# A fused GRU and transformer block: other steps and another order for the side work of the attention stage

## The reference

```python
# GRU cell, scanned over the 128 positions
r = sigmoid(i_r + h_r); z = sigmoid(i_z + h_z); n = tanh(i_n + r * h_n)
h = (1.0 - z) * n + z * h
...
x1 = ln(x) * (1.0 + scale1) + shift1
q, k, v = split(x1 @ qkv_w + qkv_b)                 # 16 heads of 128
attn = softmax(einsum("bthd,bshd->bhts", q, k) * 128 ** -0.5)
a = einsum("bhts,bshd->bthd", attn, v) @ out_w + out_b
x = x + gate1 * a
x2 = ln(x) * (1.0 + scale2) + shift2
x = x + gate2 * (gelu(x2 @ ffn_w1 + ffn_b1) @ ffn_w2 + ffn_b2)
```

## Time and profile before

| | |
|---|---|
| median of 3 runs | 740.95 us |
| the profiled execution's own time | 741.54 us |
| its span | 739.7 us |
| TensorE busy | 711.7 us |
| VectorE busy | 575.7 us |
| ScalarE busy | 484.0 us |
| GpSimd busy | 104.1 us |
| attention stage | about 271 to 655 us |

### The profile page before, as it was taken

The page is one execution under the profiler, slowest core; times in us unless marked ns, Lnnn a source line. Parts: engine busy times, 40 slices in busy tenths (PEclk is TensorE's granted clock), DMA queues, the critical chain, the costliest instruction groups (busy, mean ns, idle before and its releaser), DMA issues.

```text
span 739.7 us, 25163 instructions
## 1 busy us (share of the span) xinstructions
PE 711.7 (96%) x10380; PEld 525.0 (71%) x10380; DVE 575.7 (78%) x1581; ACT 484.0 (65%) x1621; POOL 104.1 (14%) x134
## 2 busy tenths in 40 slices
PE   6889999999999999999999999999999999999997
PEld 5689888888888776666767667676676777644555
DVE  5667888888888878877878988888887888834643
ACT  4346666666655567776787777877777777775453
POOL 0222222222210001011001111011110111000040
PEclk9869999999999999999999999999999999999999
DMA  6311111211000302322222332223322233200001
GB/s 224 96 38 39 40 39 43 70 39 39 10 12 3 116 4 44 45 44 45 45 58 46 71 52 51 55 48 71 54 51 47 56 66 44 51 16 28 29 9 50
DMA packets 79017, 36.70 MB, mean 50 GB/s; under 512 B 70667, under 2 KB 73911, under 8 KB 78903
## 3 DMA queue, kind: packets, MB, share of 16 engines
q1 hardware_dynamic: 78327, 33.53, 20.4%
q10 hardware_dynamic: 576, 1.57, 0.6%
HBM read 16.20 MB, written 2.10 MB: 25 GB/s over the span
## 4 chain that ended last, share of the span: by engine, by line
PE 83%; DVE 6%; ACT 5%; DMA 2%; SPq 2%; issue 1%; POOL 0%; DVEq 0%; ACTq 0%
PE bank L527 20%; PE bank L529 19%; PE bank L528 19%; PE bank L635 12%; PE bank L643 5%; PE bank L547 5%; SPq L381 2%; DVE h_hi L1330 2%; ACT prob L1111 1%; PE bank L534 1%; ACT zg L1037 1%; DMA pT_lo<-p_lo 1%; DVE nu L1324 1%; DMA xr<-in_weights 1%; DVE mx L1402 1%
## 5 line engine op out<-in xcount | busy, mean ns | idle before, releaser
L635 PE MATMUL bank<-h_hi,whh_hi 128*128 128x16 f16 x1536 | 111.5, 178 | 8.6 <-DVE h_hi L1330 7.2
L635 PEld LDWEIGHTS bank<-h_hi,whh_hi 128*128 128x128 f16 x1536 | 90.0, 97 | 30.2 <-DVE h_hi L1330 26.0
L635 PE MATMUL bank<-h_hi,whh_lo 128*128 128x16 f16 x1536 | 109.9, 177 | 1.5 <-issue 1.5
L1111 ACT ACTIVATE prob<-bank,nmx 128x128 f32<-128x128 f32 x256 | 90.6, 367 | 30.7 <-DVE nmx L1405 30.4
L527 PE MATMUL bank<-y_hi,w_hi 128*128 128x256 f16 (+3 forms) x344 | 108.9, 319 | 1.0 <-DVE qk_lo L1308 0.8
L529 PE MATMUL bank<-y_lo,w_hi 128*128 128x256 f16 (+3 forms) x344 | 109.1, 319 | 0.0
L528 PE MATMUL bank<-y_hi,w_lo 128*128 128x256 f16 (+3 forms) x344 | 109.1, 319 | 0.0
L635 PEld LDWEIGHTS bank<-h_hi,whh_lo 128*128 128x128 f16 x1536 | 89.7, 96 | 1.7 <-issue 1.6
L527 PE MATMUL bank<-w_hi,y_hi 128*128 128x128 f16 x512 | 89.1, 219 | 0.6 <-DVE v_lo L1409 0.6
L528 PE MATMUL bank<-w_hi,y_lo 128*128 128x128 f16 x512 | 89.1, 219 | 0.0
L529 PE MATMUL bank<-w_lo,y_hi 128*128 128x128 f16 x512 | 89.1, 219 | 0.0
(11 more groups left out here) (174 smaller groups left out, 2187.2 us busy)
## 6 DMA issues: line engine op xcount, KB each, us to landing
stage<-in_weights SPq DMA_DIRECT2D x12, 512.0 KB, 3.9
x<-in_x SPq DMA_DIRECT2D x16, 128.0 KB, 3.8
xr<-in_weights SPq DMA_DIRECT2D x4, 512.0 KB, 5.7
xr<-in_weights SPq DMA_DIRECT2D x8, 256.0 KB, 2.9
out<-xr SPq DMA_DIRECT2D x3, 512.0 KB, 3.1
xr<-in_ada_r SPq DMA_DIRECT2D x1, 1024.0 KB, 5.9
pT_hi<-p_hi SPq DMA_TRANSPOSE x64, 2.4
pT_lo<-p_lo SPq DMA_TRANSPOSE x64, 2.4
```

The lines of the kernel that those rows point to most:

```text
L635: nc.tensor.matmul(out(m0 + m), half[:, k, (m0 + m) * P:(m0 + m + 1) * P], h_hi[:, k * B:(k + 1) * B, 1], start=False, stop=False, skip_gr ...
L1111: op = nc.scalar.activation(prob[:, j, :], bank[3][:, j * T:(j + 1) * T], ACT.Exp, bias=nmx[:, j:j + 1], scale=SCALE, accum_out=den[:, j:j ...
```

## The change

Four tables have other numbers, and the cast of a weight chunk stands in front of `prob_high` in ScalarE's step, where it stood behind the late item's cast:

```diff
-ISSUED = {5: 3, 7: "4q", 8: "4k", 9: "5q", 10: "5k", 12: "rest"}
-LATER = {4: 2, 6: 3, 8: "4q", 9: "4k", 10: "5q", 11: "5k", 13: "rest"}
+ISSUED = {5: 3, 7: "4q", 9: "4k", 10: "5q", 12: "5k", 13: "rest"}
+LATER = {5: 2, 7: 3, 9: "4q", 10: "4k", 12: "5q", 13: "5k", 15: "rest"}
...
-OUT_HIGH = {5: 2, 7: 3, 9: 4, 11: 5, 12: 6, 14: 7}
-FF_LOAD = {g * H + i: (g - 1) * 3 + n for g in range(1, NG) for n, i in enumerate((1, 5, 9)) if (g - 1) * 3 + n < FF_CHUNKS}
-FF_HIGH = {d + 2: c for d, c in FF_LOAD.items()}
+OUT_HIGH = {4: 2, 6: 3, 8: 4, 11: 5, 13: 6, 14: 7}
+FF_HIGH = {H + 8 + d: c for c, d in enumerate((0, 3, 8, 16, 19, 24, 32, 35))}
+FF_LOAD = {d - 2: c for d, c in FF_HIGH.items()}
 FF_LOW = {d + 1: c for d, c in FF_HIGH.items()}
-REST_AT, SUM_AT, LOW_AT = 5, 11, 15
+REST_AT, SUM_AT, LOW_AT = 5, 13, 15
...
                     value_high(d)
+                if d in OUT_HIGH:
+                    out_high(OUT_HIGH[d])
+                elif d in FF_HIGH:
+                    ff_high(FF_HIGH[d])
                 prob_high(d - 1)
...
                     ahead_high(LAST[LATER[d]])
-                if d in OUT_HIGH:
-                    out_high(OUT_HIGH[d])
-                if d in FF_HIGH:
-                    ff_high(FF_HIGH[d])
                 attend_high(d - 2)
```

## The result

The changed kernel takes 752.86 us (median of 4 runs, 750.02 to 754.21), the kernel before 740.23 us in the same comparison: a ratio of 1.0167, 95% interval 1.0142 to 1.0192. It is slower by 12.6 us; 753.0 was predicted.

What follows compares the result with a forecast made beforehand. TensorE, busy 711.7 of 739.7 us, was taken as the bound, so only its stalls count; 9.0 + 3.05 + 0 = +12.1 on the profiled 741.54 gave 753.6, or 753.0 by the median; 8-in-10 range 746 to 758.

Steps and rivals of the forecast that it cites:

- part 1: Feed-forward chunks cast ahead of p: p waits for late loads, eight projections stall; +9.0 us, bounds +4 to +15.
- part 2: Attention-output chunks and late items: items drained where the next is issued stall TensorE; +3.05 us, bounds -1 to +4.
- some 10 us more of TensorE's wait on aT_lo: Expected in the changed profile at eight projections, one step after each feed-forward cast.
- the stall of 0.95 at step 5: TensorE's stall at 299.05 us, claimed to go because step 4 loses its late item; -0.95 us.
- Rival 1: Feed-forward chunks cost nothing, in time or taken by slack; only part 2 is left, 744 us; chance 0.07.
- Rival 2: Not slower: casts fill ScalarE's idle, new drain-and-issue meetings cost nothing; 738.5 us, decided at steps 5, 7, 24; chance 0.05.
- Rival 3: Lateness not swallowed: late p pushes transposes past the attend; 1.9 us a chunk, +18 with part 2, 759 us; chance 0.10.
- The page's estimate of a load: 2.6 us for a 256 KB chunk, taking 0.3 off each, 2.4 in all; the prediction used the trace's 2.8 to 2.9.
- Steps 5, 7 and 13: Attention steps where a late item is drained as the next is issued; new stalls of +1.45, +1.55 and +1.0 us.
- The cancellation of steps 8 and 9: Step 8 loses a small stall and step 9 may get one; set against each other, 0.
- Casts ahead of p at nothing: Attention-output casts wait for nothing, ScalarE's 0.4 to 0.5 us before p_hi covers them; charged 0, at most 0.52 lag.
- Part 3: GpSimd's sums moved from i = 11, 12 to 13, 14; valued at 0, bounds -1.6 to +0.5 us.

Runs made afterwards that it cites:

- e1: Kernel before with only the feed-forward part: new steps of load and cast, cast ahead of p; 748.44 us against 739.38, ratio 1.0134.
- e2: Kernel before with only the change's late items and output chunks, output casts ahead of p; 743.24 us, ratio 1.0066.
- e5: Kernel before with one number changed: late item 2 drained in step 5, not step 4; 740.67 us against 740.44, ratio 1.0009.
- e7: Kernel before with only GpSimd's sums moved, to i = 13 and 14; 739.58 us against 740.44, ratio 0.9991.
- e6: Changed kernel, feed-forward loads three steps ahead, no item issued in a drain's step unless late queries cover it; 738.24 us against 740.44 before, ratio 0.9972.
- e9: e6 with the weight casts back behind p; 736.96 us against 740.44 for the kernel before, ratio 0.9957.

## Why the prediction was right

Time and mechanism were right: forecast +12.1, measured +12.6 by medians and by the ledger. That it came so near is partly luck: by the ledger, part 1 was set 0.3 too high and part 2 0.85 too low.

- *Which stalls decide.* Right: the waits on aT_lo and qk_lo carry the whole difference, and no engine has more work. One sign was overstated: the prediction wanted some 10 us more of TensorE's wait on aT_lo, and the view has 6.6 more (2.5 to 9.1). Its own sum gave no more than 8.05, since the stall of 0.95 at step 5 goes, and the view leaves out the first 0.16 of each stall.
- *Part 1, +9.0.* The ledger has +8.7, of it 8.3 in the stalls that were forecast; the experiment e1 has +9.1. Landing 4.2 us after the second transpose was 4.1; p_hi's lateness, forecast at 2.0, was 1.9 (it starts 4.64 behind the second transpose, 2.74 before), and VectorE idles 1.98 for it; the 0.6 that VectorE's idle before the maximum would swallow is the 0.51 that is gone there. The stall forecast at 1.25 for step 24 is 1.10. Rival 1 fell by e1. Rival 2 fell in the places that it named, steps 5, 7 and 24, with stalls of 1.58, 1.58 and 1.10. Rival 3 fell by the transposes: over the whole stage they hold TensorE for 1.6 us of drawn idle, against 1.0 before, where it needed some 6 more. Once it did what rival 3 says: behind chunk 43 the late p holds up the attend as well, by the 0.44 at 539.74, where the prediction saw no second stall.
- *The page's estimate of a load,* 2.6 us by "DMA: Bandwidth & Descriptors", section "Anatomy of one DMA", in the Trainium skill, would have made part 1 6.6. The traces before and after have 2.8 to 2.9 for this issue path, and the measurement decides.
- *Part 2, +3.05.* The ledger has +3.9 and so has e2. Steps 5, 7 and 13 are each within 0.15 of what was said. Two small terms were off: the stall of 0.95 does not go as a whole, since the attend that follows then waits for its transposes (0.3 us in the changed kernel, 0.40 in e5), and two stalls on the transposes came at steps 7 and 9 (0.38 at 311.61, 0.23 at 325.27). The first of these is no doing of the items: e1 and e7, which have them as before, have it too (0.33 and 0.38). The cancellation of steps 8 and 9 itself held: 0.29 went, 0.15 came.
- *Casts ahead of p at nothing.* Right in size (e2, and e6 against e9), and it was no gain either. The cover that the prediction named, an idle of 0.4 to 0.5 us in front of p_hi, is there before the change in three of the six steps only (4, 13 and 14); p_hi at 306.34, 318.20 and 340.46 (steps 6, 8 and 11) has no idle in front. So the slack that took the casts there must lie further on; where, was not followed up.
- *Part 3 at 0.* Right by e7's stalls, 10.8 us against 10.4. The rule of the Trainium skill, "SBUF — State Buffer", section "Who interferes with whom", is borne out in what it says of the two engines: the pair took 1.25 us beside the sum, 0.73 without, and of the 1.25 the first scaling alone had 0.93 and ended 0.15 behind the sum's end. A gain of 1.6 us in time did not come of it in the stalls, because VectorE was not what p waited for; e7's time alone would not exclude it.

## What to carry to other kernels

In an engine that works in order, the place of an instruction that may wait for a DMA is worth as much as what stands behind it (here some 5 us for the place, 8.7 for the load's step, of 740): put it behind the work that others need, or issue the load so early that it never waits. Compare the landing time, counted from the queue entry in front of the load, with the moment the engine gets there. With one buffer for a chain of items, look at where an item is drained against where the next is issued, and keep a block of other work of the consumer's between them.

## What the runs showed of the hardware

VectorE's subtraction `xr<-xn,xr`, with both inputs in SBUF, took 1.22 us beside a GpSimd subtraction and 0.68 without. In the changed kernel, which has GpSimd's chunk in another step, it takes 0.68 in all six places of the three groups:

```profile
392.10 0.68 DVE L1440 TENSOR_TENSOR xr<-xn,xr 128x512 f32<-128x512 f32 x1
394.15 0.68 DVE L1440 TENSOR_TENSOR xr<-xn,xr 128x512 f32<-128x512 f32 x1
```

Before, the second of them:

```profile
392.11 1.22 DVE L1440 TENSOR_TENSOR xr<-xn,xr 128x512 f32<-128x512 f32 x1
```

GpSimd's own 1.16 and 1.27 us are the same with and without. It had not been in the sum. No stall of TensorE hung on it: before, there is none between 388.35 and 432.81.

Most of the DMA transposes on SyncE's queue take 1.19 to 1.22 us of the queue each, but 15 to 21 of the 128 take 1.4 to 2.7. In all ten traces these belong to heads with odd numbers, and one of the two is long for heads 3, 5, 25, 33, 41, 43, 49, 51, 53, 57, 59 and 61 in every one of the ten. Several of TensorE's small stalls of 0.2 to 0.9 us on pT_lo stand behind such a one. What lengthens them was not tried.
